# Two-layer attention block with matmuls added while the weights load, and newly drawn instruction orders

## The reference

```
# layer 0, 8 heads of 32 (linear attention)
xn = ln(x, ln_w, ln_b)
q  = softmax over the features of a head (xn @ Wq + bq)
k  = softmax over the tokens (xn @ Wk + bk + (1 - mask) * -1e6)
v  = (xn @ Wv + bv) * mask
y  = q @ (k^T v)                                  per head
scale, shift = split(silu(emb) @ W_emb + b_emb)
x  = x + silu(ln(y, ln2_w, ln2_b) * (1 + scale) + shift) @ W_out + b_out

# layer 1, 16 heads of 16 (softmax attention)
xn = ln(x);  q, k, v = xn @ q_w + q_b, ...
y  = softmax(q k^T + mask) v                      per head
x  = x + silu(ln(y) * (1 + scale) + shift) @ out_w + out_b
```

## Time and profile before

| what | value |
|---|---|
| median of 3 runs | 878.15 us (877.68 to 878.59) |
| the profiled execution's own time | 876.07 us |
| its span, first to last instruction | 873.8 us |
| PE busy | 820.7 us (94%), 8609 matmuls |
| DVE busy | 782.1 us (90%) |
| POOL busy | 734.8 us (84%) |
| ACT busy | 710.8 us (81%) |
| mean granted TensorE clock | 0.991 |

### The profile page before, as it was taken

The page is one execution under the profiler, slowest core; times in us unless marked ns, Lnnn a source line. Parts: engine busy times, 40 slices in busy tenths (PEclk is TensorE's granted clock), DMA queues, the critical chain, the costliest instruction groups (busy, mean ns, idle before and its releaser), DMA issues.

```text
span 873.8 us, 25110 instructions
## 1 busy us (share of the span) xinstructions
PE 820.7 (94%) x8609; PEld 589.1 (67%) x8609; DVE 782.1 (90%) x1609; ACT 710.8 (81%) x1250; POOL 734.8 (84%) x1214
## 2 busy tenths in 40 slices
PE   3997889999999999999999999999999999999985
PEld 2486666677777777777777777777777776655443
DVE  6797799989999999898999999999999988998953
ACT  6654929797899788989888888888888888988894
POOL 7488989898999899899999989999988977986423
PEclk9998999999999999999999999999999999999998
DMA  8211433534354253344434434444435442445401
GB/s 240 59 38 37 125 90 100 129 66 104 85 128 127 56 122 90 89 118 113 105 77 116 122 93 107 98 109 113 116 73 106 107 79 69 128 102 112 113 19 49
DMA packets 149304, 85.82 MB, mean 98 GB/s; under 512 B 87478, under 2 KB 141852, under 8 KB 149180
## 3 DMA queue, kind: packets, MB, share of 16 engines
q1 hardware_dynamic: 149180, 84.23, 39.4%
HBM read 39.52 MB, written 25.79 MB: 75 GB/s over the span
## 4 chain that ended last, share of the span: by engine, by line
PE 40%; POOL 23%; DVE 17%; issue 11%; ACT 3%; DMA 3%; SPq 2%; POOLq 0%; DVEq 0%; ACTq 0%
PE banks L687 11%; DVE NM L1263 7%; PE banks L834 5%; PE banks L695 4%; PE banks L821 3%; POOL Z L1918 3%; PE banks L810 3%; PE banks L717 3%; POOL AB L1989 3%; POOL ZHL L1925 3%; DVE st L1164 3%; PE banks L702 3%; POOL SH L1963 2%; POOL rs L1905 2%; DMA ZT<-ZHL 2%
## 5 line engine op out<-in xcount | busy, mean ns | idle before, releaser
L1263 DVE TENSOR_REDUCE NM<-banks 128x4 f32<-128x1024 f32 x256 | 302.8, 1213 | 13.7 <-PE banks L810 12.8
L1681 ACT ACTIVATE wraw<-banks,uu 128x1024 f32<-128x1024 f32 x154 | 169.6, 1137 | 20.4 <-PE banks L821 19.1
L1681 ACT ACTIVATE PX<-banks,uu 128x1024 f32<-128x1024 f32 x102 | 113.1, 1134 | 13.1 <-PE banks L821 11.5
L687 PE MATMUL banks<-wo,SH 128*128 128x256 f16 x768 | 95.7, 276 | 6.3 <-POOL SH L1963 5.8
L1905 POOL TENSOR_TENSOR rs<-ve,nhalf 128x2 f32<-128x2 f32 x128 | 90.8, 710 | 10.6
L687 PE MATMUL banks<-wv,ZT 128*128 128x256 f16 x768 | 95.9, 276 | 0.1
L821 PE MATMUL banks<-SQ,SK 53*128 53x256 f16 x1024 | 89.4, 272 | 6.2 <-DVE NM L1263 1.5
L1963 POOL TENSOR_TENSOR SH<-ST,SH 128x512 f16<-128x512 f32 x64 | 74.4, 1167 | 21.6 <-ACT SH L1649 21.5
L810 PE MATMUL banks<-SK,SQ 51*128 51x256 f16 x1024 | 87.8, 272 | 4.3 <-DVE NM L1263 3.3
L1663 ACT ACTIVATE R<-banks,fcs,sqs 128x256 f32<-128x256 f32 x128 | 74.4, 581 | 20.9 <-PE banks L695 19.9
L1925 POOL TENSOR_TENSOR ZHL<-Z,ZHL 128x256 f16<-128x256 f32 x128 | 86.4, 696 | 5.3
(11 more groups left out here) (184 smaller groups left out, 1915.9 us busy)
## 6 DMA issues: line engine op xcount, KB each, us to landing
scr<-AB SPq DMA_DIRECT2D x64, 256.0 KB, 2.5
X<-in_x_dram SPq DMA_DIRECT2D x32, 256.0 KB, 2.9
SK<-scr SPq DMA_DIRECT2D x64, 128.0 KB, 2.9
SQ<-scr SPq DMA_DIRECT2D x64, 128.0 KB, 2.8
out_dram<-wemb SPq DMA_DIRECT2D x32, 256.0 KB, 2.6
SK<-scr SPq DMA_DIRECT2D x64, 64.0 KB, 2.9
SQ<-scr SPq DMA_DIRECT2D x64, 64.0 KB, 2.8
wemb<-in_L_cond_emb_w_dram SPq DMA_DIRECT2D x1, 1024.0 KB, 5.3
```

What stands on the lines that cost most here:

```text
L687: m = PE.matmul(dst[:, t, :], zt[:, j, k, t * P:(t + 1) * P], w[:, i, k, :], start=(k, n) == (0, 0), stop=(k, n) == (1, 2))
L1263: V.tensor_reduce(NMe[:, c, :, 2 * g:2 * g + 2], banks[:, n:n + 2, :].rearrange("p a (h m) -> p a h m", m=T), AX.X, ALU.max, negate=True). ...
L1681: A.activation(px(v % 5), banks[:, n:n + 2, :].rearrange("p a n -> p (a n)"), ACT.Exp, scale=uu[:, 0:1]).then_inc(S["exp"])
```

## The change

It has two parts.

The first is a new piece on PE, hot, ahead of everything else there: 44 matmuls (HOT) of 128x128 weights with 512 columns, all into one PSUM bank that nobody reads. Their operand is the first half of the tile AB, in float16, which DVE fills with ones in a new piece hz, the first of its list. AB is written again by qa(0), so qa(0) and ka(0) on ACT get a wait for hot. tr_w1, which uses the same bank, waits for hot as well (in FREED).

The second is that the lists of all five engines, and with them BANK, FREED and SETUP, are drawn anew, with the durations of the preparation's pieces as they were seen. No piece is added but hz and hot, and none is dropped. At the start the lists differ most: ld_m stands ahead of ld_c, and ld_w1 ahead of x_in(1); z0T(0) stands directly behind the loads and ahead of x_in(2); on DVE w1m comes ahead of s0(2), and s0(2), s0(3) and s0(4) stand earlier among the wl pieces; on PE bb2 stands between ar_w1 and ar_w0, row3 behind ar_w0, rw and ar_o0 behind q0(0); on ACT fill_q0 moves to behind qt(3); on POOL r0(4) stands ahead of qs(0). From about batch 5 on the lists have the same pattern as before, with neighbours exchanged here and there.

```diff
+HOT = 44
...
 FREED = {
...
+    "ghot": "-",
-    "gt_w1": "-",
+    "gt_w1": "hot",
...
 # PE
+            def hot():
+
+                ready(e, "hz")
+                clear(e, "ghot", 0)
+                h = AB[:, 0, 0].rearrange("p a t -> p (a t)")
+                for i in range(HOT):
+                    m = PE.matmul(banks[:, home("ghot"), :], h[:, 0:P], h, start=True, stop=True)
+                m.then_inc(C["PE"])
...
-            pm(); tr_w1(); bb0(); cnd_t(); tr_w0(); ar_w1(); row3(); ar_w0(); bb2(); fx1(); tr_o0(); fx0()
-            ar_o0(); fm1(); rw(); q0(0); fm0(); bb1(); k0(0); v0(0); tr_f0(); q0(1); k0(1); ktT(0); v0(1); v0(2)
-            ar_f0(); qtT(0); att(0); q0(2); y0(0); ktT(1); k0(2); att(1); qtT(1); q0(3); y0(1); y0T(0); ktT(2)
-            q0(4); col(); tr_f1(); qtT(2); k0(3); o0(0); y0T(1); tr_o1(); ar_o1(); tr_b(); att(2); v0(3); k0(4)
-            y0(2); qtT(3); ar_b(); o0(1); ktT(3); v1p(0); q1p(0); k1p(0); y0T(2); k0(5); att(3); q0(5); qtT(4)
+            hot(); pm(); tr_w1(); cnd_t(); bb0(); tr_w0(); ar_w1(); bb2(); ar_w0(); row3(); fx1(); fx0(); bb1()
+            fm1(); fm0(); tr_o0(); q0(0); rw(); v0(0); ar_o0(); k0(0); q0(1); tr_f0(); k0(1); qtT(0); ktT(0)
+            ar_f0(); v0(1); att(0); q0(2); v0(2); y0(0); ktT(1); k0(2); att(1); qtT(1); q0(3); y0(1); y0T(0)
+            qtT(2); v0(3); col(); q0(4); ktT(2); o0(0); y0T(1); k0(3); att(2); tr_b(); k0(4); ktT(3); tr_o1()
+            y0(2); ar_o1(); ar_b(); v0(4); qtT(3); att(3); v1p(0); o0(1); tr_f1(); q1p(0); y0T(2); ar_f1(); y0(3)
...
 # DVE
+            def hz():
+                V.memset(AB[:, 0, 0], 1.0).then_inc(C["DVE"])
...
-            s0(0); s0(1); mb0(); csl_(); s0(2); w1m(); w0m(); mx_w1(); o0m(); mx_w0(); w1p(); w0p(); wl_q1()
-            s0(3); wl_v1(); mx_o0(); wl_k0(); wl_q0(); s0(4); o0p(); f1m(); wl_v0(); q1(0); f0m(); qm(0); km(0)
+            hz(); mb0(); csl_(); s0(0); s0(1); w1m(); w0m(); mx_w1(); mx_w0(); w1p(); w0p(); o0m(); s0(2); wl_q1()
+            wl_v1(); s0(3); wl_k0(); s0(4); wl_v0(); wl_q0(); f1m(); q1(0); mx_o0(); qm(0); wl_k1(); f0m(); km(0)
...
 # ACT
-                first(e, b, "fcs")
+                first(e, b, "fcs", "hot")
...
-            th(); fill_k0(); fill_k1(); csT_(); bc0(); wh_q1(); wh_v1(); pa(); wh_k0(); wh_q0(); pc(); fy1()
-            p3_(); wh_v0(); mc(); fy0(); fill_q0(); perm(); wh_k1(); bc1(); ke(0); kt(0); qe(0); wh_o0(); qt(0)
+            th(); fill_k0(); fill_k1(); csT_(); wh_q1(); bc2(); pa(); wh_v1(); pc(); wh_k0(); wh_v0(); fy1()
+            bc0(); wh_q0(); fy0(); p3_(); wh_k1(); perm(); qe(0); bc1(); ke(0); mc(); qt(0); kt(0); ke(1); qe(1)
...
 # POOL
-            cst(); r0(0); r0(1); z0(0); z0(1); xb0(0); xb0(1); pb(); nmz(); r0(2); pd(); z0(2); r0(3); v1z()
-            qs(0); r0(4); z0(3); qs(1); z0(4); qs(2); r1(0); yn0(0); qs(3); r1(1); sl0(0); yn0(1); qs(4); xb0(2)
+            cst(); r0(0); r0(1); z0(0); xb0(0); xb0(1); z0(1); pb(); pd(); r0(2); r0(3); z0(2); r0(4); nmz()
+            v1z(); qs(0); z0(3); z0(4); qs(1); qs(2); r1(0); yn0(0); qs(3); r1(1); sl0(0); yn0(1); qs(4); xb0(2)
...
 # SP
-            x_in(0); ld_c(); ld_m(); x_in(1); ld_w1(); x_in(2); ld_w0(); ld_o0(); ld_r(); ld_f1(); ld_f0(); mbd0()
-            x_in(3); x_in(4); am(0); am(1); ld_o1(); z0T(0); am(2); z0T(1); aug_d(); z0T(2); z0T(3); am(3); am(4)
+            x_in(0); ld_m(); ld_c(); ld_w1(); x_in(1); ld_w0(); ld_o0(); ld_r(); ld_f1(); ld_f0(); z0T(0); x_in(2)
+            x_in(3); x_in(4); mbd0(); ld_o1(); aug_d(); am(0); am(1); am(2); z0T(1); am(3); z0T(2); z0T(3); z0T(4)
```

More of the change, by code:

```diff
@@ L67 @@
+    "gpv2": "26062742211234662012561171340346",
+    "gc6": "22424024226042226464604402000064",
+    "gc7": "04440402044604200246640646626002",
+    "gpv3": "47224600210204477132302160001457",
+    "gty0": "70362625226744707054272560251560",
+    "gty1": "44201640613117470102602774304471",
+    "gy1T": "70256314316565060134701753512322",
+    "go1": "12707410174262112122114057404300",
+    "ghot": "0",
+    "gpm": "1",
+    "grow3": "6",
+    "gcnd": "2",
     "gcol": "1",
-    "grw": "5",
-    "gbb0": "2",
@@ L70 @@
-    "gbb1": "1",
-    "gbb2": "2",
+    "grw": "6",
+    "gbb0": "3",
+    "gbb1": "0",
+    "gbb2": "5",
     "gt_w0": "4",
[L73 to L78, removed]
+    "ga_w0": "4",
+    "gt_w1": "0",
+    "ga_w1": "0",
+    "gt_o0": "4",
+    "ga_o0": "4",
+    "gt_o1": "3",
     "ga_o1": "1",
     "gt_f0": "0",
[L81 to L86, removed]
@@ L87 @@
-    "gfm0": "0",
-    "gfx1": "4",
-    "gfm1": "4",
+    "ga_f0": "2",
+    "gt_f1": "7",
+    "ga_f1": "0",
+    "gt_b": "5",
+    "ga_b": "3",
+    "gfx0": "2",
+    "gfm0": "3",
+    "gfx1": "0",
+    "gfm1": "2",
 }
@@ L94 @@
     "gk0": (
-        "f1m bc1 qt:1 at:1 at:3 qa:1 max:8 max:9 yt:1 exp:10 th0:8 exp:30 yt:17 qa:9 ka:10 max:71 x1:13 ka:13 "
-        "max:96 max:104 o:11 o:12 x1:19 exp:124 max:144 exp:140 yt:74 exp:157 o:19 qt:29 o:21 yt:93 "),
+        "q1:1 f0m qt:1 kt:3 th0:2 vt:1 qa:3 max:10 yt:1 exp:10 o:1 yt:13 max:47 max:56 o:5 x1:12 x1:13 max:87 o:9 "
+        "max:104 max:112 max:119 Y1:28 exp:124 th0:22 max:152 yt:74 exp:157 max:176 qt:29 o:21 exp:188 "),
     "gkt": (
-        "ke:1 ke:2 bc2 Y0:3 Y0:4 ka:2 Y0:6 th0:5 ke:9 Y1:3 ke:11 max:42 max:51 th1:5 exp:55 exp:63 ke:17 yt:39 "
@@ L254 @@
     "PE": (
-        "pm tr_w1 bb0 cnd tr_w0 ar_w1 row3 ar_w0 bb2 fx1 tr_o0 fx0 ar_o0 fm1 rw fm0 bb1 tr_f0 ar_f0 col tr_f1 "
-        "tr_o1 ar_o1 tr_b ar_b ar_f1 ").split(),
+        "hot pm tr_w1 cnd bb0 tr_w0 ar_w1 bb2 ar_w0 row3 fx1 fx0 bb1 fm1 fm0 tr_o0 rw ar_o0 tr_f0 ar_f0 col "
+        "tr_b tr_o1 ar_o1 ar_b tr_f1 ar_f1 ").split(),
     "DVE": (
-        "mb0 csl w1m w0m mx_w1 o0m mx_w0 w1p w0p wl_q1 wl_v1 mx_o0 wl_k0 wl_q0 o0p f1m wl_v0 f0m wl_k1 mx_f0 "
-        "film0 wl_o0 bm o1m mx_o1 mx_b fcs o1p mx_f1 film1 wl_o1 ").split(),
+        "hz mb0 csl w1m w0m mx_w1 mx_w0 w1p w0p o0m wl_q1 wl_v1 wl_k0 wl_v0 wl_q0 f1m mx_o0 wl_k1 f0m mx_f0 "
+        "o0p film0 wl_o0 bm o1m mx_o1 mx_b fcs mx_f1 o1p film1 wl_o1 ").split(),
     "ACT": (
-        "th fill_k0 fill_k1 csT bc0 wh_q1 wh_v1 pa wh_k0 wh_q0 pc fy1 p3 wh_v0 mc fy0 fill_q0 perm wh_k1 bc1 "
-        "wh_o0 bc2 fill_q1 wh_o1 ").split(),
+        "th fill_k0 fill_k1 csT wh_q1 bc2 pa wh_v1 pc wh_k0 wh_v0 fy1 bc0 wh_q0 fy0 p3 wh_k1 perm bc1 mc "
+        "wh_o0 fill_q0 fill_q1 wh_o1 ").split(),
     "POOL": (
-        "cst pb nmz pd v1z mb1 ").split(),
+        "cst pb pd nmz v1z mb1 ").split(),
 }
```

804 lines of the change are left out of this document (394 added, 410 removed), and 192 rows, old and new, of the table FREED.

## The result

The median of 14 executions is 872.2 us (867.81 to 876.92), that of the kernel before, run 14 times beside it, 877.36. The ratio is 0.9943, 95% interval 0.9928 to 0.9958: 5.2 us less, faster by more than the 0.2% that counts. The forecast was 870.1 in 863 to 876.5. The changed kernel was run a second time, on another occasion, 12 times beside 35 of the kernel before: 873.47 against 876.73, ratio 0.9966 (0.9954 to 0.9978), 3.3 us less. The intervals only just touch; the gain is 3 to 5 us, where 8.0 were forecast. All runs named here are of the fast state.

A forecast was written before the change was run, and what follows sets the result against it. PE was taken to bound 150 to 820 us, with idle and low clock before that to be won. Part 2's -6.5 and Part 3's -1.5 make -8.0 on the 878.15 median: 870.1 us, range 863 to 876.5.

The forecast's parts named there:

- What bounds: PE sets 150 to 820 us at 98% busy; what can go lies before 150: idle, gaps and slow-clock matmuls.
- Part 1: Hot's 44 matmuls at the start: eight at half clock, then full, ending at 12.5 us without delaying w0m.
- Rival (b): Clock falls back in the sparse pieces behind hot; 2.5 to 3.5 us of gain lost, 873.5 to 876 us; 20%.
- The point on transposes: In the preparation behind hot: transposes don't count as clock activity, by the skill's text, which would give Rival (b)'s time.
- Part 2: Preparation's path with new order and clock: q0(0) at 33, qs(0) at 38.0, 5.8 us earlier; -6.5 us taken.
- Part 3: 65 to 150 us: waits at ar_o1 and ar_b now stand together; -1.5 us, bounds -8 and +4.
- Part 4: The rest, redrawn order of the middle and the tail: 0 us, with -3 to +5 for the order.
- Rival (c): Something else (x landing, p3 to aug_d, POOL) carries the path by 44 us; gain 1.5 us or less, 877; 9%.
- (a): Gaps and falls of the clock to 150 us largely vanish, another 5 to 8 us gained: 863 us; 12%.
- (d): New order of the middle is slower, one more PE wait of 0.4 us per batch: 881 us; 9%.
- (e): At the start hot stays at half clock and ends at 20.2 us, q0(0) near 41: 881 us; 3%.

The follow-up runs named there:

- x6: Changed kernel with POOL's fill of V1 (v1z) moved from ahead of qs(0) to behind qs(1); 872.96 us, ratio 0.9966 to the kernel before.
- x11: Changed kernel with POOL's fill of V1 cut into twelve pieces at the same place; 873.22 us, ratio 0.9967 to the kernel before.
- x1: Kernel before with only hz, hot and the waits for hot added, lists as they were; 873.37 us, ratio 0.9975 to the kernel before.
- x4: Changed kernel with 20 matmuls in hot in place of 44; 875.42 us, ratio 0.9998 to the kernel before.
- x3: Changed kernel with HOT = 40 and four extra matmuls behind each of cnd_t, tr_w0 and ar_w0; 873.56 us, ratio 0.9966 to the kernel before.
- x7: x3 with the fill of V1 also moved behind qs(1) on POOL; 876.04 us, ratio 0.9988 to the kernel before.
- x9: The changed kernel unaltered, run a second time; 873.47 us, ratio 0.9966 to the kernel before.
- x13: Changed kernel with the fill of V1 in twelve pieces behind qs(1), plus the filler matmuls of x8; 874.63 us, ratio 0.9975 to the kernel before.
- x8: Changed kernel with unread filler matmuls, 9 ahead of rows(0,4) and 8 ahead of o0(3); 872.64 us, ratio 0.9961 to the kernel before.
- x14: x13 with the extra warm matmuls of x3 as well; 876.69 us, ratio 0.9997 to the kernel before.

## Why the prediction was right, and where its size was off

- **The size as a whole.** 3.3 to 5.2 us came of 8.0. In the terms of the first profile: 4.66 at qs(0), -0.3 from there to rows(0,0), -0.2 behind that and 0.5 outside the span make 4.7 (876.07 to 871.39). The second profile is of the other course: 3.31 at qs(0), -2.6 to rows(0,0), 0.9 behind that, in all 1.6 of span. As far as one profile of each tells, that as much as 5.2 came in the first set had some luck in it.
- **What bounds.** Right. The 13 us of idle PE at the start and its low clock could be used, and 150 to 820 us stayed as it was.
- **Part 1.** hot began at 1.44 (1.1 to 1.5 said). The weight loads of hot stood 0.43 us apart until 6.5, then 0.22:

```profile
6.11 0.15 PEld L934 LDWEIGHTS banks<-AB 128*128 128x128 f16 x1 [0.28 <-issue]
6.54 2.51 PEld L934 LDWEIGHTS banks<-AB 128*128 128x128 f16 x12 [0.28 <-issue]
```

  That is twelve slow matmuls, not eight, and the end at 13.6 instead of 12.5 us. In x6 and x11 the step came at 4.4, in x1 at 4.75, in x4 at 5.2, in x3 and x7 at 5.6, in x9 and x13 at 6.5, in x8 and x14 at 7.4: 2.9 to 6.0 us behind hot's start. The 3.4 us taken from the falls lies in this, and 5.1 us was what came; it isn't fixed within 3 us. The later end was not free on PE. The prediction looked at tr_w1 and w0m, not at tr_w0 behind them: w0m was through at 14.4, not 16.4, and tr_w0, behind hot and bb0 in PE's queue, ran at 16.18, so that DVE idled 1.63 us for it. In x6, where hot ended at 12.5, tr_w0 ran at 15.29. But w0p ended at 22.2 to 22.3 in both. bb0 took 1.13 us, as said.
- **Rival (b)** was given 20% and came about as a mechanism: bb2 took 1.97 + 1.21 = 3.2 us, to the tenth what (b) says. Its price was set a little high: w0p ended at 22.3, not 23.5, and q0(0) came at 34.09, not 35. Of six executions of this part of the list, the changed kernel, x9, x13, x6, x8 and x11, three lost the clock near 16.8, and three kept it past bb2: x11 until 18.0, x6 until 21.4, x8 throughout. q0(0) came at 34.1 in the first three, at 31.7 to 32.4 in the others. By medians the changed kernel gained 5.2 and 3.3 us, where (b), taken off the same base, says 2 to 4.6 and the forecast 8.0. The outcome lies between, and the second time in (b). The point on transposes that the prediction weighs isn't decided: x3_warm kept the clock with twelve ordinary matmuls between, but x8 kept it with the very pieces, transposes included, with which the changed kernel lost it.
- **Part 2.** The term that was mis-sized: -6.5 (of which -5.8 at qs(0) itself, the rest for r0(4) being done), measured at qs(0) -4.66 in the first profile and -3.31 in the second. q0(0) at 34.09 instead of 33 is the fall of the clock. DVE was not late: z0T(0) took 2.50 us to issue and not 1.35, x(2) was issued at 21.55, and DVE idled 1.78 us for it, but wl_q0 was through at 32.1, not 33.1. x3_warm with q0(0) at 32.24 has the same qs(0), so q0(0) doesn't decide; what does is POOL's queue, as the prediction reckoned, 1.1 us later than its 38.0, or, in the other draw, the hold of f1m. This hold is what the prediction missed. The step read "q1(0) follows f1m (2.4 us)" and took from the trace how long f1m lasts, but not that one of its steps, be1c, lasted 1.68 us beside POOL's fill and 0.17 without it.
- **Part 3.** -1.5 forecast. From qs(0) to rows(0,0) the changed kernel lost 0.3 us in the first profile and 2.6 in the second. The wait at ar_o1 and ar_b did go, as said:

```profile
PE banks L873 <- DVE mxd L1316: 0.9, 1, 0.9
```

  0.9 us, where it was 3.7, and with it the fall in the earlier trace rows; the clock is 1.00 from 65 to 109. It brought nothing that the marks show; POOL has 42.06 of 45 us of work there. The row of POOL was in the prediction, as the reason against more; it was reason against 1.5 too. The fall near 110 us stayed; in x8, without it, PE was 1.1 to 1.9 us earlier at 116 us, counted from rows(0,0), and 0.1 to 0.9 at 120.
- **Part 4.** 0 forecast. From rows(0,0) to the end of the span 764.5 us before, 764.7 and 763.6 after. Right, within a scatter of 5 us over all profiles.
- **Rival (c)**, something else carries the path, 9%: half true. POOL does from 36 us on, which caps what the clock can bring. **(a), (d), (e)** did not come: the gaps from 65 to 150 us are 14.4 us, where they were 12.9, PE has 98% of the middle, hot was at full clock by 6.5.

Left open: why x7 and x14, where the clock is kept up and qs(0) is early, have medians 3.1 and 2.1 us above x6 and x13, which are the same without the warm matmuls. rows(0,0) doesn't show it (106.71 and 107.47, 107.78 and 108.38). What x7's profile lost against x6's lies behind rows(0,0) (767.6 against 762.5 us to the end), and PE is busy 655.87 us of 145 to 816, in x6's 658.89; single executions differ by as much, and no cause was found. Nor was it tried what the time would be with the hold excluded for certain, for instance by a fill on another engine.

## What to carry to other kernels

A low clock at the start can be worked off with idle matmuls, if they end right where the first dependent piece begins; in the kernel where they ended 6 us earlier the clock was down again and the time was that of before. The short pieces behind them can lose the clock again. Before pricing such a gain, look which engine's queue is next: here q0(0) 1.85 us earlier moved qs(0) by 0.08, because of POOL's queue. And look in the trace of before for instructions of one form whose time is five or ten times the usual: what holds them is not a semaphore, no wait names it, and a new order can move it onto the path.
